# A fourth slot for the 0/1 adjacency, made in the round's second unit in place of its fifth

## The chip, the cores and the metric

The kernel runs on one core of one Trainium2 chip. Its metric is device time in microseconds (us). TensorE multiplies matrices (PE in the profile, its weight loads PEld), VectorE (DVE), ScalarE (ACT) and GpSimd (POOL) work element by element, and SyncE (SP) only issues transfers. Each engine runs its own list of instructions in order and waits on semaphores for the others.

## The reference

There are 16 graphs (batches) of 512 nodes with 128 features. A first stage mixes neighbours with the row-normalised adjacency, adds the input and normalises; five gated layers then pass messages over the 0/1 adjacency; a last residual and normalisation follow.

```python
adj_norm = adj / (jnp.sum(adj, axis=-1, keepdims=True) + EPS)
h = relu(concat([x, adj_norm @ x]) @ weight + bias)
x = layernorm(x + h)
A = (adj != 0).astype(x.dtype)
h = x
for l in range(5):
    m = h @ weight[l]
    agg = einsum('bij,bid->bjd', A, m)
    h = gru_cell(agg, h, w_ih, w_hh, b_ih, b_hh)   # gates r, z, n; h = (1 - z) * n + z * h
x = layernorm(x + h * mask)
```

## The kernel before

**Units and rounds.** One layer of one batch is a unit. A round (a `window` in the code) has five slots, and three batches are in flight: `UNITS = ((0, 0), (1, 2), (2, 4), (0, 1), (1, 3))` gives for each slot (rounds back, layer). So the first unit of a round is layer 0 of the youngest batch, the second layer 2 of the batch before, and so on. Beside its five units a round prepares the next batch (its first stage) and finishes an old one (its last normalisation, from round 3 on). Rounds -1, 0 and 1 are the ramp and have an order of their own; rounds 3 to 14 are one loop body, run twelve times; four rounds at the end are written out again. Every engine's list is written by hand inside `window`, slot by slot, and nothing else sets the order.

**A unit, by engine.** PE adds up the neighbours: four matmuls of `edges` with `tok_hi` (L1001) and four with `tok_lo` (L1006) into `ps_tok`. It then makes nine matmuls of the state with the recurrent weights into `ps_hn`, `ps_r`, `ps_z` (the helper at L893 to L895, called by `state_products`), turns the next unit's state into `ps_tok` (four transposes, L888) and makes nine matmuls of the aggregate with the input weights (L893 to L895 again). ACT takes `agg_hi` out of `ps_tok`, DVE makes `agg_lo` from it (L661), ACT makes `r_gate` (L635) and `z_gate` (L645), DVE `r_hn` (L874) and `n_pre` (L774), ACT `n_gate` (L573), POOL `z_h` (L495), DVE `zm_n` (L807) and the new `h` (L829). ACT rounds `h` to `h_hi`, POOL makes the rest `h_lo` (L485, for a new batch L490). DVE's tail of a unit (`n_pre`, `zm_n`, `h`) stands at the start of the next slot. Before the turn PE waits for `agg_lo`; before the aggregation it waits for `tok_lo`, and for a layer 0 also for the batch's `edges`, `x1_hi` and `x1_lo`.

**The 0/1 adjacency.** `edges_of` (L733) writes `edges` in four pieces of 128x512 from `adj_in` (`not_equal` 0) with DVE, into a ring of three slots, one for each batch in flight: slot `batch % RING`. In the rounds from 2 on it stands behind `h` in the fifth slot (slot 4), after the old batch's last aggregation has been waited for. In the ramp it stands in other places. PE takes the ring's slots of the batches in flight by three numbers (`ring`).

**Around the new place.** In slot 1 of a round DVE makes, behind `h`: the four pieces of `pre2` (L744), four `stats2` (L760), `row_eps` (128x4, L847), `mv2` (L753), `var2` (128x4, L755), then `tok_lo` of the unit in slot 2 (L661). ACT reads `adj_in` for the row sums in the same slot (L542). In slot 0 DVE also makes `xt_lo` (L661), and POOL `adjt_lo` (L438) behind `z_h`.

**Transfers.** SP loads, in this order in a round, the next inputs `xt_in` (after `xt_lo`) and `adjt_in` (after `adjt_lo`), stores the finished output, loads `x_in` (after `pre1`), and last `adj_in`, after the row sums and `edges`.

Of the kernel before, what the change touches and what calls it, by code (L numbers as in the profile page):

```python
# [22 lines left out]
LAST = UNITS.index((2, LAYERS - 1))  # L23
# [151 lines left out]
def program(nc, x, xt, adj, adjt, mask, w0, b0, wlt, wiht, whht, gru_b, out):  # L175
    B, N, D = x.shape
    C = N // P
# [3 lines left out]
    with ExitStack() as ctx:  # L181
        def sb(name, shape, dtype=F32):
            return ctx.enter_context(nc.sbuf_tensor(name, shape, dtype))
# [4 lines left out]
        def sem(name):  # L188
            return ctx.enter_context(nc.semaphore(name))
# [24 lines left out]
        adjt_in = sb("adjt_in", [P, C, N])  # L214
        xt_in = sb("xt_in", [P, N])
        x_in = sb("x_in", [P, C, D])
        RING, KEPT = 3, 4
        edges = sb("edges", [P, RING, C, N], F32R)
        x1_kept = sb("x1_kept", [P, KEPT, C, D])

# [56 lines left out]
        s_adj_in = sem("s_adj_in")  # L277
# [42 lines left out]
        s_agg = sem("s_agg")  # L320
# [337 lines left out]
        def _(dve):  # L658
# [9 lines left out]
            def weights():  # L668
                dve.wait_ge(s_small, 2 * 16)
                nc.vector.tensor_tensor(rz_bias[:], bih_cols[:, 0:2], bhh_cols[:, 0:2], ALU.add).then_inc(s_whh, 1)  # L670
                dve.wait_ge(s_weights, 3 * 16)
                nc.vector.tensor_copy(whh_hi[:], whh_t[:]).then_inc(s_whh, 1)
                dve.wait_ge(s_whh, 2)
                low_part(whh_lo[:], whh_t[:], whh_hi[:]).then_inc(s_whh, 1)
                for l in range(LAYERS):
                    dve.wait_ge(s_wc_hi, l + 1)
                    low_part(wc_lo[:, l, :], product_bank[l][:, 0:G * D], wc_hi[:, l, :]).then_inc(s_wc_lo, 1)

            def window(w):
# [15 lines left out]
                def mean_parts():  # L695

                    dve.wait_ge(s_nsum_tok, w.prepared(1, 1))
                    dve.wait_ge(s_rinv, w.prepared(2, 2))
                    for c in range(C):
                        last = nc.vector.scalar_tensor_tensor(  # L700
                            out=mixed[:, c, :], in0=ps_b[0][:, c * D:(c + 1) * D],
                            scalar=row_inv[:, c:c + 1], in1=own[:, c, :], op0=ALU.mult, op1=ALU.add)
                    last.then_inc(s_mixed, 1)
# [16 lines left out]
                def moments1():  # L720

                    for c in range(C):
                        nc.vector.bn_aggr(mv1[:, c, :], stats1[:, c, :]).then_inc(s_mv1, 1)
                    dve.wait_ge(s_mv1, w.prepared(C, C))
                    nc.vector.tensor_scalar(var1[:], mv1[:, :, 1], LN_EPS, None, ALU.add).then_inc(s_var1, 1)  # L725
# [5 lines left out]
                def edges_of(cs):  # L731
                    for c in cs:
                        nc.vector.tensor_scalar(edges[:, bass.ds(ring, 1), c, :].rearrange("p o m -> p (o m)"),  # L733
                                                adj_in[:, c, :], 0.0, None, ALU.not_equal).then_inc(s_edges, 1)
# [28 lines left out]
                if w.prepares():  # L763
                    ring = dve.snap(w.batch(-1) % RING)
# [3 lines left out]
                for slot in range(SLOTS):  # L768
# [57 lines left out]
                    if w.unit_before(slot):  # L826
                        dve.wait_ge(s_zh, w.units(slot))
                        dve.wait_ge(s_zm1n, w.units(slot))
                        nc.vector.tensor_tensor(h[made][:], z_h[:], zm1_n[:], ALU.subtract).then_inc(s_h, 1)  # L829
                    if w.first == -1 and slot == 1:  # L830
                        weights()
                    if w.prepares():
                        if slot == 2 and not w.leads():
                            mean_parts()
                        if slot == 3 and not w.ramps():
                            moments1()
                        if slot == 4 and not w.ramps():

                            dve.wait_ge(s_agg, w.units(LAST + 1))
                            edges_of(range(C))  # L840
                    if slot == 1 and w.finishes() and not w.idles():
                        pre2_of_batch()
                        if slot == w.end_slot():
# [34 lines left out]
                    if slot == 1 and w.ramps() and w.first != 0:  # L878

                        edges_of(range(2) if w.first == -1 else range(C))  # L880

            all_windows(window, dve)


        @block.tensor
        def _(pe):
# [21 lines left out]
            def window(w):  # L908
# [37 lines left out]
                    gs = slice(g * D, (g + 1) * D)  # L946
                    return split_product(dst[:], weights_hi[:, gs], weights_lo[:, gs], hi[:], lo[:], start, stop)

                ring = [pe.snap(w.batch(back) % RING) if w.first - back >= 0 else None for back in range(RING)]

                def edges_from(c, back):

# [31 lines left out]
                for slot in range(SLOTS):  # L984
# [72 lines left out]
                    if slot == 1 and w.leads():  # L1057
                        sums_by_tokens()
                        if w.first == -1:
# [4 lines left out]
                            own_products(1)  # L1064

            all_windows(window, pe)


# [34 lines left out]
```

## Time and profile before

| | us |
|---|---|
| median of 3 runs | 680.66 |
| lowest and highest | 679.27, 681.64 |
| profiled execution, span from first to last instruction | 678.2 |
| PE busy | 621.9 (92%) |
| DVE busy | 568.8 (84%) |
| ACT busy | 416.0 (61%) |
| POOL busy | 390.5 (58%) |
| one round in the loop (the same instruction of two rounds, 320.79 and 360.09) | 39.3 |

The profiled span is 2.5 us under the median of the runs; a sum made on the trace is carried over to the median by adding that. The granted TensorE clock of the span is 0.984 of full speed, and 1.00 in the rounds that are looked at below. In a timeline a duration includes the time that an issued instruction is held at an operand, so one form of instruction with two durations is a sign of being held.

### The profile page before, as it was taken

Reading aid. Unit: us, or ns where it says so; the run is one execution under the profiler, and the core shown is the slowest. Engines: PE = TensorE matmul, PEld = TensorE weight load, DVE = VectorE, ACT = ScalarE, POOL = GpSimd, SP = SyncE. Lnnn points to the kernel's source line nnn. Section 1 sums busy time; section 2 is a strip of 40 time slices with the busy share of each in tenths; the row PEclk is TensorE's granted clock in tenths of the full one; section 3 lists DMA queues with packets and bytes.
Section 4 is the critical chain, followed back from the end, with each engine's and each line's share of the span. In section 5 each row is a group of like instructions: output and inputs, shape, how many; then the busy total and the mean of one; then the engine's idle time right before and its main releaser. Section 6 shows DMA issues by size and latency. Waiting matters only on the chain.

```text
span 678.2 us, 10100 instructions
## 1 busy us (share of the span) xinstructions
PE 621.9 (92%) x2922; PEld 496.0 (73%) x2922; DVE 568.8 (84%) x1153; ACT 416.0 (61%) x775; POOL 390.5 (58%) x309
## 2 busy tenths in 40 slices
PE   4588899999999999999999999999999999999973
PEld 3467677787877778787777878777787878778852
DVE  1867877989899898989989898998989899886664
ACT  3557385766757576675757667575766667555431
POOL 3526373664757566475767657566765747546252
PEclk9799999999999999999999999999999999999987
DMA  7351302221212222221222221131222111000001
GB/s 226 132 163 40 116 17 78 79 78 51 104 31 84 86 77 77 69 86 31 96 75 77 77 84 71 31 113 57 77 77 92 62 31 62 15 0 16 1 16 31
DMA packets 37424, 47.28 MB, mean 70 GB/s; under 512 B 1409, under 2 KB 18945, under 8 KB 37409
## 3 DMA queue, kind: packets, MB, share of 16 engines
q1 hardware_dynamic: 36368, 46.27, 20.5%
q10 hardware_dynamic: 944, 0.72, 0.3%
q0 software_dynamic: 96, 0.10, 0.2%
q8 instruction: 7, 0.11, 0.1%
q14 instruction: 9, 0.07, 0.0%
HBM read 42.90 MB, written 4.19 MB: 69 GB/s over the span
## 4 chain that ended last, share of the span: by engine, by line
PE 57%; DVE 28%; issue 9%; ACT 4%; DMA 2%; DVEq 1%; POOLq 0%; SPq 0%; ACTq 0%
PE ps_tok L1001 8%; PE ps_tok L1006 7%; DVE edges L733 5%; PE ps_tok L888 4%; DVE r_hn L874 3%; PE ps_r L893 3%; PE ps_r L894 3%; PE ps_b L894 3%; PE ps_b L893 3%; PE ps_r L895 3%; PE ps_b L895 3%; PE ps_z L893 3%; PE ps_z L895 3%; PE ps_z L894 3%; DVE zm_n L807 3%
## 5 line engine op out<-in xcount | busy, mean ns | idle before, releaser
L485 POOL TENSOR_TENSOR h_lo<-h,h_hi 128x512 fp32r<-128x512 f32 x64 | 84.2, 1315 | 108.2 <-ACT h_hi L522 108.2
L495 POOL TENSOR_TENSOR z_h<-z_gate,h 128x512 f32<-128x512 f32 x80 | 104.8, 1310 | 47.2 <-ACT z_gate L645 47.2
L438 POOL TENSOR_TENSOR adjt_lo<-adjt_in,adjt_hi 128x512 fp32r<-128x512 f32 x64 | 95.1, 1508 | 31.3 <-ACT adjt_hi L522 31.3
L1001 PE MATMUL ps_tok<-edges,tok_hi 128*128 (+1 forms) x320 | 92.2, 411 | 17.7 <-DVE edges L733 15.3
L522 ACT ACTIVATE tok_hi<-ps_tok 128x512 fp32r<-128x512 f32 x64 | 38.3, 599 | 108.6 <-PE ps_tok L888 108.5
L573 ACT ACTIVATE n_gate<-n_pre,gru_bias 128x512 f32<-128x512 f32 x80 | 57.7, 722 | 63.4 <-DVE n_pre L774 63.4
L1006 PE MATMUL ps_tok<-edges,tok_lo 128*128 (+1 forms) x320 | 88.4, 399 | 0.0
L1001 PEld LDWEIGHTS ps_tok<-edges,tok_hi 128*128 128x128 f32 x320 | 59.0, 191 | 38.7 <-issue 22.9
L829 DVE TENSOR_TENSOR h<-z_h,zm_n 128x512 f32<-128x512 f32 x80 | 85.2, 1065 | 0.8
L807 DVE SCALAR_TENSOR_TENSOR zm_n<-z_gate,n_gate 128x512 f32<-128x512 f32 x80 | 66.2, 828 | 22.1 <-ACT n_gate L573 20.1
L874 DVE SCALAR_TENSOR_TENSOR r_hn<-ps_hn,gru_bias,r_gate 128x512 f32<-128x512 f32 x80 | 59.5, 744 | 27.2 <-ACT r_gate L635 27.0
L1006 PEld LDWEIGHTS ps_tok<-edges,tok_lo 128*128 128x128 f32 x320 | 60.8, 190 | 14.7
L522 ACT ACTIVATE h_hi<-h 128x512 fp32r<-128x512 f32 x80 | 50.2, 628 | 20.9 <-DVE h L829 20.7
L635 ACT ACTIVATE r_gate<-ps_r,rz_bias 128x512 f32<-128x512 f32 x80 | 54.9, 687 | 12.4 <-PE ps_r L895 9.7
L774 DVE TENSOR_TENSOR n_pre<-ps_in,r_hn 128x512 f32<-128x512 f32 x80 | 55.3, 692 | 8.1
L661 DVE TENSOR_TENSOR tok_lo<-ps_tok,tok_hi 128x512 fp32r<-128x512 f32 x64 | 44.1, 688 | 19.7 <-ACT tok_hi L522 19.4
L522 ACT ACTIVATE agg_hi<-ps_tok 128x512 fp32r<-128x512 f32 x80 | 48.0, 600 | 19.5 <-PE ps_tok L1006 18.5
L661 DVE TENSOR_TENSOR agg_lo<-ps_tok,agg_hi 128x512 fp32r<-128x512 f32 x80 | 54.5, 682 | 3.7 <-ACT agg_hi L522 3.4
L645 ACT ACTIVATE z_gate<-ps_z,rz_bias 128x512 f32<-128x512 f32 x80 | 55.1, 689 | 0.4
L444 POOL TENSOR_TENSOR rstd<-var,minus_half 128x4 f32<-128x4 f32 x16 | 16.2, 1011 | 55.8 <-DVE var L725 55.7
L888 PE MATMUL ps_tok<-ident,h 128*128 128x128 f32 x256 | 39.9, 278 | 9.0 <-DVE h L829 7.3
L888 PEld LDWEIGHTS ps_tok<-ident,h 128*128 128x128 f32 x256 | 29.4, 140 | 24.2 <-DVE agg_lo L661 9.5
(123 smaller groups left out, 1603.3 us busy)
## 6 DMA issues: line engine op xcount, KB each, us to landing
adjt_in<-in_adj_t_dram SPq DMA_DIRECT2D x16, 1024.0 KB, 5.2
adj_in<-in_adj_dram SPq DMA_DIRECT2D x16, 1024.0 KB, 5.2
xt_in<-in_x_t_dram SPq DMA_DIRECT2D x16, 256.0 KB, 2.8
x_in<-in_x_dram SPq DMA_DIRECT2D x16, 256.0 KB, 2.7
out_dram<-y_out SPq DMA_DIRECT2D x16, 256.0 KB, 2.3
wl_t<-in_wl_t_dram ACTq DMA_DIRECT2D x1, 320.0 KB, 5.4
wih_t<-in_w_ih_t_dram ACTq DMA_DIRECT2D x1, 192.0 KB, 3.0
whh_t<-in_w_hh_t_dram ACTq DMA_DIRECT2D x1, 192.0 KB, 9.3
```

What stands on the lines that cost most here:

```text
L438: nc.gpsimd.tensor_tensor(adjt_lo[:, j, :], adjt_in[:, j, :], raw(adjt_hi[:, j, :]), ALU.subtract).then_inc(s_adjt_lo, 1)
L485: nc.gpsimd.tensor_tensor(h_lo[made][:], h[made][:], raw(h_hi[made][:]), ALU.subtract).then_inc(s_h_lo, 1)
L495: nc.gpsimd.tensor_tensor(z_h[:], z_gate[:], h[layer][:], ALU.mult).then_inc(s_zh, 1)
L522: return nc.scalar.activation(dst, src, ACT.Copy)
L661: return nc.vector.tensor_tensor(dst, src, raw(hi), ALU.subtract)
L807: nc.vector.scalar_tensor_tensor(out=zm1_n[:], in0=z_gate[:], scalar=1.0, in1=n_gate[:], op0=ALU.subtract, op1=ALU.mult).then_inc(s_zm1n, 1)
L829: nc.vector.tensor_tensor(h[made][:], z_h[:], zm1_n[:], ALU.subtract).then_inc(s_h, 1)
L874: nc.vector.scalar_tensor_tensor(out=r_hn[:], in0=ps_hn[:], scalar=bhh_cols[:, 2:3], in1=r_gate[:], op0=ALU.add, op1=ALU.mult).then_inc(s_ ...
L888: return nc.tensor.transpose(dst, src, ident[:])
L893: nc.tensor.matmul(dst, lhs_hi, rhs_hi, start=start, stop=False)
L1001: nc.tensor.matmul(ps_tok[:], tok_hi[:, c * P:(c + 1) * P], edges_from(c, unit[0]), start=c == 0, stop=False)
L1006: last = nc.tensor.matmul(ps_tok[:], tok_lo[:, c * P:(c + 1) * P], edges_from(c, unit[0]), start=False, stop=c == C - 1)
```

## The change

The ring `edges` gets four slots. In the rounds from 2 on, DVE writes the next batch's `edges` in slot 1, behind `h` and ahead of `pre2`, where it stood in slot 4 behind `h`. What it waits for changes with it: for the load of `adj_in` by name, and for the last aggregation of the batch that had the ring's slot before, which was in the round before. PE still takes three numbers of the ring, now modulo 4. SP's order of transfers is not touched.

```diff
-        RING, KEPT = 3, 4
+        RING, KEPT = 4, 4
...
+                    if w.prepares() and slot == 1 and not w.ramps():
+
+                        dve.wait_ge(s_adj_in, w.prepared(16, 16))
+                        if w.first >= 3:
+                            dve.wait_ge(s_agg, w.last_layers())
+                        edges_of(range(C))
...
-                        if slot == 4 and not w.ramps():
-
-                            dve.wait_ge(s_agg, w.units(LAST + 1))
-                            edges_of(range(C))
...
-                ring = [pe.snap(w.batch(back) % RING) if w.first - back >= 0 else None for back in range(RING)]
+                ring = [pe.snap(w.batch(back) % RING) if w.first - back >= 0 else None for back in range(3)]
```

DVE's list in the loop, slot 1, before:

```order
L829 TENSOR_TENSOR h<-z_h,zm_n 128x512 [waits s_zm1n,s_zh]
L738 REGISTER_ALU
L744 ISA [waits s_cent2,s_x1_kept,s_last]
L744 SCALAR_TENSOR_TENSOR pre<-ps_b,mask_cols,x_kept 128x128
```

and now:

```order
L829 TENSOR_TENSOR h<-z_h,zm_n 128x512 [waits s_zm1n,s_zh]
L832 ISA
L834 REGISTER_ALU [waits s_adj_in]
L733 ISA [waits s_agg]
L733 TENSOR_SCALAR edges<-adj_in 128x512
L733 ISA
L733 TENSOR_SCALAR edges<-adj_in 128x512
L733 ISA
L733 TENSOR_SCALAR edges<-adj_in 128x512
L733 ISA
L733 TENSOR_SCALAR edges<-adj_in 128x512
L738 REGISTER_ALU
```

The four pieces of `edges` now stand between `h` and `pre2`, and so ahead of `row_eps`, `var2` and the `tok_lo` of slot 2. DVE's list at the end of the loop body, slot 4, before:

```order
L829 TENSOR_TENSOR h<-z_h,zm_n 128x512 [waits s_zm1n,s_zh]
L733 ISA [waits s_agg]
L733 TENSOR_SCALAR edges<-adj_in 128x512
L733 ISA
L733 TENSOR_SCALAR edges<-adj_in 128x512
L733 ISA
L733 TENSOR_SCALAR edges<-adj_in 128x512
L733 ISA
L733 TENSOR_SCALAR edges<-adj_in 128x512
L874 SCALAR_TENSOR_TENSOR r_hn<-ps_hn,gru_bias,r_gate 128x512 [waits s_r]
```

and now:

```order
L661 TENSOR_TENSOR agg_lo<-ps_tok,agg_hi 128x512 [waits s_agg_hi]
L829 TENSOR_TENSOR h<-z_h,zm_n 128x512 [waits s_zm1n,s_zh]
L876 SCALAR_TENSOR_TENSOR r_hn<-ps_hn,gru_bias,r_gate 128x512 [waits s_r]
```

There `r_hn` follows `h` directly. The lists of PE, ACT, POOL and SP keep their order.

## Rows read from the trace of the kernel before

**Rows 1.** The page's first part: busy time, share of the span, instructions.

```profile
PE 621.9 (92%) x2922; PEld 496.0 (73%) x2922; DVE 568.8 (84%) x1153; ACT 416.0 (61%) x775; POOL 390.5 (58%) x309
```

**Rows 2.** Waits of the whole span: who waited for whom, us, times, longest.

```profile
PEld ps_tok L1001 <- issue: 22.9, 24, 1.7
...
PE ps_tok L1001 <- DVE edges L733: 15.3, 13, 1.2
```

**Rows 3.** Timeline of PE, round's end and next slot 0: start, us, instruction.

```profile
348.34 1.09 PE L1001 MATMUL ps_tok<-edges,tok_hi 128*128 x4
...
350.20 0.39 PE L893 MATMUL ps_hn<-h_hi,whh_hi 128*128 128x512 f32 x1
...
361.31 0.39 PE L895 MATMUL ps_in<-agg_hi,wc_lo 128*128 128x512 f32 x1
362.89 1.19 PE L1001 MATMUL ps_tok<-edges,tok_hi 128*128 x4 [1.19 <-DVE edges L733]
...
364.85 0.39 PE L893 MATMUL ps_hn<-h_hi,whh_hi 128*128 128x512 f32 x1
...
366.92 0.65 PE L888 MATMUL ps_tok<-ident,h 128*128 128x128 f32 x4
```

**Rows 4.** Timeline of DVE over the same slot 0.

```profile
358.64 1.53 DVE L829 TENSOR_TENSOR h<-z_h,zm_n 128x512 f32<-128x512 f32 x1
360.09 2.50 DVE L733 TENSOR_SCALAR edges<-adj_in 128x512 f32 x4
362.52 0.74 DVE L874 SCALAR_TENSOR_TENSOR r_hn<-ps_hn,gru_bias,r_gate 128x512 f32<-128x512 f32 x1
...
363.97 1.62 DVE L661 TENSOR_TENSOR xt_lo<-xt_in,xt_hi 128x512 fp32r<-128x512 f32 x1
365.51 0.68 DVE L807 SCALAR_TENSOR_TENSOR zm_n<-z_gate,n_gate 128x512 f32<-128x512 f32 x1
366.12 0.68 DVE L661 TENSOR_TENSOR agg_lo<-ps_tok,agg_hi 128x512 fp32r<-128x512 f32 x1
```

**Rows 5.** Timeline of ACT over the same slot 0.

```profile
361.22 0.68 ACT L635 ACTIVATE r_gate<-ps_r,rz_bias 128x512 f32<-128x512 f32 x1
...
362.88 0.63 ACT L522 ACTIVATE xt_hi<-xt_in 128x512 fp32r<-128x512 f32 x1
364.09 0.72 ACT L573 ACTIVATE n_gate<-n_pre,gru_bias 128x512 f32<-128x512 f32 x1 [0.57 <-DVE n_pre L774]
```

**Rows 6.** Timeline of POOL over the same slot 0.

```profile
360.91 1.40 POOL L485 TENSOR_TENSOR h_lo<-h,h_hi 128x512 fp32r<-128x512 f32 x1 [1.29 <-ACT h_hi L522]
362.50 1.29 POOL L490 TENSOR_TENSOR h_lo<-h,h_hi 128x512 fp32r<-128x512 f32 x1 [0.18 <-ACT h_hi L522]
363.74 1.31 POOL L495 TENSOR_TENSOR z_h<-z_gate,h 128x512 f32<-128x512 f32 x1
```

**Rows 7.** The lines of `edges` at 360 and `adjt_lo` at 333: min/median/max ns.

```profile
L733 DVE TENSOR_SCALAR edges<-adj_in x4: 411/412/1493, 360.1 to 361.1; 128x512 f32 x4
...
L438 POOL TENSOR_TENSOR adjt_lo<-adjt_in,adjt_hi x2: 1283/1511/1739, 333.2 to 334.4; 128x512 fp32r<-128x512 f32 x2
```

**Rows 8.** Timeline of all engines, slot 1 and the start of slot 2.

```profile
333.51 1.51 DVE L807 SCALAR_TENSOR_TENSOR zm_n<-z_gate,n_gate 128x512 f32<-128x512 f32 x1
...
336.64 1.11 DVE L744 SCALAR_TENSOR_TENSOR pre<-ps_b,mask_cols,x_kept 128x128 f32<-128x128 f32 x4
...
338.79 0.17 DVE L847 TENSOR_SCALAR row_eps<-row_sum 128x4 f32<-128x4 f32 x1
...
339.24 1.29 POOL L485 TENSOR_TENSOR h_lo<-h,h_hi 128x512 fp32r<-128x512 f32 x1 [3.07 <-ACT h_hi L522]
339.27 1.28 DVE L755 TENSOR_SCALAR var<-mv 128x4 f32<-128x4 f32 x1
...
340.47 0.68 DVE L661 TENSOR_TENSOR tok_lo<-ps_tok,tok_hi 128x512 fp32r<-128x512 f32 x1
```

**Rows 9.** Timeline of PE and of its weight loads there.

```profile
341.10 0.39 PE L895 MATMUL ps_in<-agg_hi,wc_lo 128*128 128x512 f32 x1
341.34 1.19 PE L1001 MATMUL ps_tok<-edges,tok_hi 128*128 x4
...
341.33 0.53 PEld L1001 LDWEIGHTS ps_tok<-edges,tok_hi 128*128 128x128 f32 x3 [0.28 <-issue]
```

## The prediction

> **What bounds the kernel now.** I read the page's busy times first: PE is busy for 621.9 of 678.2 us [rows 1], so the end can only come earlier by way of PE's gaps. The waits come second. In the middle of the run one gap has the change's name on it: PE waits for `edges` 13 times, 15.3 us in all, once for each `edges` that is made in a slot 4 [rows 2]. The timelines of one round come third. PE issues the last matmul of slot 4 at 361.31; the next one would follow 0.24 later, at 361.55, as matmuls of this form do in a row (341.10 to 341.34 in [rows 9]). It begins at 362.89 [rows 3], so the gap costs 1.34 us a round, and 13 of them 17.4 us. That is the most that this edit can give back at this place.
>
> **Part 1: the gap in slot 0.** With `edges` gone from DVE's list, PE begins the aggregation at 361.55. Its eight matmuls take 1.86 us (348.34 to 350.20 [rows 3]), so it is at the state products at 363.41. There it needs the new batch's `h_lo` from POOL, which ends at 362.50 + 1.29 = 363.79 [rows 6]. That `h_lo` follows ACT's chain behind DVE's `h`, which ended ahead of `edges`, so it comes no earlier. PE begins the state products at about 363.87, against 364.85, and has them done 2.07 later (364.85 to 366.92 [rows 3]), at 365.94. The turn that follows waits for `agg_lo`, and here the gain is lost. Line by line:
> - `r_hn` waits for `r_gate`, which ends at 361.22 + 0.68 = 361.90 [rows 5]; it starts at 361.96 in place of 362.52 [rows 4]. Only 0.56 us of the 2.50 us of `edges` comes back, since ACT was not ready.
> - `xt_lo` comes 1.45 behind `r_hn` (362.52 to 363.97), so at 363.41, but `xt_hi` ends at 363.51 [rows 5]: 363.55.
> - Now DVE and POOL meet. In [rows 8] `zm_n` takes 1.51 us where it takes 0.68 in [rows 4], under POOL's first `adjt_lo`, and POOL's second one takes 1.739 us where the first took 1.283 [rows 7]. So DVE's instruction was held until the first ended, went next, and held the second for 0.46. They take turns. By this `xt_lo`, queued at 363.55, goes when `h_lo` ends at 363.79, and is done at 364.33 (in the trace it ended 0.54 after the end of `z_h`: 363.97 + 1.62 against 363.74 + 1.31). `z_h` is held for 0.46 and ends at 365.51 instead of 365.05.
> - `n_gate` takes 0.72 [rows 5] and is ready at 364.27; `zm_n` comes when `z_h` is already next in turn, so it is held until 365.51 and ends some 0.56 later, 366.07, against 366.19 before. `agg_lo` follows 0.61 behind: 366.68 against 366.80 [rows 4].
> So PE turns at 366.80 instead of 366.92: **0.12 us a round**. If `z_h` goes ahead of `xt_lo`, both are as before and the gain is 0. Were DVE never held behind `z_h`, `agg_lo` would be done before 365.94 and the gain 366.92 - 365.94 = 0.98. I take 0.12, the value that the turns in [rows 7, 8] give, and keep 0 and 0.98. For 13 rounds: -1.6 us (0 to -12.7).
>
> The Trainium skill ("SBUF — State Buffer", section "Who interferes with whom") says that VectorE and GpSimd share one pair of ports by an exclusive lock for an instruction with two SBUF inputs or in a two-port mode, and that the one that issues first keeps it to its end. The held `zm_n` agrees with that. By that rule `zm_n` can't pass `z_h`, and the gain of this part is the 0.12 or 0.
>
> **Part 2: `edges` in slot 1.** It stands behind `h`, so from 336.64, where `pre2` starts now [rows 8]. Of the four pieces in [rows 7] three take 0.41 us; the fourth, 1.49 us, is held by POOL's `h_lo` at 360.91. The pieces start 0.34 apart (360.1 to 361.1 for four), so four that are not held push back what follows by 1.36 us. POOL is idle here until its `h_lo` at 339.24 (3.07 us idle before it [rows 8]), so they are not held, and cost 1.36 instead of 2.50. The two waits in front of them are for things long done: the load of `adj_in`, which ACT reads earlier in the same slot, and an aggregation of the round before. Behind them in DVE's list stand `pre2`, `stats2`, `row_eps`, `mv2`, `var2` and `tok_lo`.
> - `row_eps` moves from 338.79 to 340.15. POOL's `h_lo` runs from 339.24 to 340.53. `var2`, the same operation and size, took 1.28 us under it where `row_eps`, ahead of it, took 0.17 [rows 8]; now `row_eps` is the one that is held, until 340.53, and ends at about 340.65, 1.69 later than now (338.96).
> - `mv2` follows, and `var2` comes when POOL is idle and takes 0.17 instead of 1.28. Now `tok_lo` ends at 340.47 + 0.68 = 341.15. From `row_eps` to `var2` it is 0.48 (338.79 to 339.27); counted from 340.57, where the held one would have started unheld, `var2` is at about 341.0, `tok_lo` starts 0.1 behind it and ends at 341.75. So 1.1 of the 1.69 us disappears in the wait of `var2`, which was there anyway, and **0.60 us** is left.
> - PE waits for this `tok_lo`. Its weight load for slot 2 starts at 341.33, after a gap of 0.28, and 0.18 behind `tok_lo`; the matmul before was issued at 341.10 and the next is due at 341.34 [rows 9]. There is no slack. The 24 gaps in the row of [rows 2] that says "issue" are two for each of 12 rounds, 1.91 a round: one in slot 0 and this one. So a later `tok_lo` delays PE one for one.
> Only rounds with `pre2` in slot 1, 3 to 14, have this queue: 12 x 0.60 = +7.2 us. The bounds are 0.27 if the small `row_eps` is not held after all (`var2` then starts at 340.63 and `tok_lo` ends at 341.42) and 0.9 if `cent2` and `y_out` of POOL in slot 2 also come to lie before DVE's `zm_n` and `h` and delay the next `tok_lo`: 12 x 0.27 = +3.2, 12 x 0.9 = +10.8. I take 0.60, by the row of the held `var2`.
>
> What of it comes back later in the round? PE has no other gap in slots 2 to 4 that is larger than some 0.2 us, and DVE's later chain hangs on PE's turn in slot 2 by way of `tok_hi` and `r_gate`, so both are late by the same amount when slot 0 comes. Nothing is given back.
>
> **Part 3: what costs nothing.** The ring of four needs memory, not time; PE's list keeps its order and its three register numbers. The `adj_in` load can leave right behind the `x_in` load in slot 3 instead of in the next slot 0. Nobody waits for it in either place: its next reader is a slot 1. It would lie beside other work, and I count 0. The Trainium skill (same page, section "SBUF: two separate sides") says that a transfer can't be slowed by a compute operation nor the other way round. The same 0 would result; no row here isolates it.
>
> **The sum.** -1.6 + 7.2 = +5.6 us on the profiled 678.2: 683.8. The median of the runs lies 2.5 above that span, so 686.3 us, which is 0.8% more. The measurement tells about 0.3%, or 2 us, from no change.
>
> **Rivals.**
> 1. *The gap really closes (faster).* If DVE's `zm_n` gets in ahead of `z_h`, slot 0 gives 0.98 a round, 12.7 in all, and even with the cost of part 2 it is 680.66 - 12.7 + 7.2 = 675.2. For it speaks that `n_gate` is ready at 364.27, just when `xt_lo` ends; against it that `z_h` is by then queued for half a microsecond, and the held and holding pairs of [rows 7, 8]. From a gain of 0.72 a round on (12 x 0.60 + 2.0 over 13) the kernel is faster.
> 2. *The cost in slot 1 is mostly hidden (no change).* If a 128x4 `row_eps` slips through under `h_lo`, the cost is 3.2 and the sum +1.6: 682.3. Against it stands `var2` at 1.28 us, for it that this one starts in the middle of POOL's instruction and not 0.03 behind its start.
> 3. *More than one `tok_lo` is late (slower still).* DVE's `zm_n` in slot 2 slides behind POOL's `cent2` and its `h` behind `y_out`; then `tok_lo` of slot 3 is late too. At 0.9 a round and no gain in slot 0 it is +10.8: 691.5.
> 4. *The edit doesn't do what it says.* PE would go on waiting for `edges` 13 times. The order of DVE's list excludes it: the pieces are 20 us ahead of their reader. I give it none.
>
> **Chances.** Forecast 0.60, rival 1 0.16, rival 2 0.14, rival 3 0.10. The forecast's own range, with 0 to 0.12 in slot 0 and 0.5 to 0.7 in slot 1, is 685 to 689. The range for 8 in 10 reaches down to rival 1 and up to near rival 3: 675 to 690. Slower by over 0.3%: forecast, rival 3 and no more, less a little for a forecast that falls short: 0.67. Within: 0.17. Faster: 0.16.
>
> **What would show it.** In the profile after, PE's wait for `edges` is gone; in its place PE waits in slot 0 for POOL's `h_lo` (0.4 to 0.5 us) and before the turn for `agg_lo` (about 0.9 us), and `z_h` of slot 0 takes 1.7 to 1.8 us instead of 1.31. In slot 1 four `edges` take about 0.41 us each, `row_eps` about 0.5 us or is seen as held, `var2` 0.17, and PE's gap ahead of slot 2 grows from 0.28 to 0.8 or 0.9. The round is 39.8 us long instead of 39.3. I am wrong if `zm_n` in slot 0 ends less than 1.6 us after PE's state products began (2.2 by the forecast, 1.0 by rival 1), or if the gap ahead of slot 2 does not grow.

## The result and the profile after

The changed kernel takes 685.26 us in the median (684.75 to 686.6, four runs), the kernel before 681.07 in the same runs; the ratio is 1.0079 with a 95% interval of 1.0057 to 1.0101. It is slower by 4.2 us in the medians; the interval allows 3.9 to 6.9 us. The profiled execution spans 683.7 us against 678.2.

First the busy times and PE's waits over the whole span (us, times, longest).

```profile
PE 628.1 (92%) x2922; PEld 497.3 (73%) x2922; DVE 556.0 (81%) x1153; ACT 414.2 (61%) x775; POOL 397.2 (58%) x309
```

```profile
PE ps_tok L890 <- DVE agg_lo L661: 6.8, 13, 0.6
PE ps_tok L1003 <- DVE tok_lo L661: 6.3, 14, 1.4
PE ps_hn L895 <- POOL h_lo L490: 4.6, 13, 0.4
```

The 13 waits for `edges` of [rows 2] are gone, with 15.3 us. In their place stand two waits in slot 0, for `h_lo` and for `agg_lo`, and one in slot 2, for `tok_lo`. DVE is busy for 12.8 us less than in the kernel before, mainly since four `edges` take 1.42 us where they took 2.50, and the kernel is slower all the same. (The new code is two lines longer, so L888, L893, L1001 and L874 of before are L890, L895, L1003 and L876 here.)

Slot 0, on PE, then DVE, then POOL, to be laid beside [rows 3, 4, 6]:

```profile
365.17 1.10 PE L1003 MATMUL ps_tok<-edges,tok_hi 128*128 x4
...
367.56 0.49 PE L895 MATMUL ps_hn<-h_hi,whh_hi 128*128 128x512 f32 x1 [0.36 <-POOL h_lo L490]
...
370.41 0.65 PE L890 MATMUL ps_tok<-ident,h 128*128 128x128 f32 x4 [0.51 <-DVE agg_lo L661]
```

```profile
365.57 0.75 DVE L876 SCALAR_TENSOR_TENSOR r_hn<-ps_hn,gru_bias,r_gate 128x512 f32<-128x512 f32 x1 [1.76 <-ACT r_gate L635]
...
367.18 0.79 DVE L661 TENSOR_TENSOR xt_lo<-xt_in,xt_hi 128x512 fp32r<-128x512 f32 x1
...
367.90 1.78 DVE L807 SCALAR_TENSOR_TENSOR zm_n<-z_gate,n_gate 128x512 f32<-128x512 f32 x1
```

```profile
366.13 1.29 POOL L490 TENSOR_TENSOR h_lo<-h,h_hi 128x512 fp32r<-128x512 f32 x1 [0.29 <-ACT h_hi L522]
...
367.39 1.74 POOL L495 TENSOR_TENSOR z_h<-z_gate,h 128x512 f32<-128x512 f32 x1
```

PE begins the aggregation on time (365.17), and turns 5.24 us later. Before, the matmul was due at 361.55 and the turn began at 366.92, 5.37 us later [rows 3]. So 0.13 us is gained where 1.34 us of gap was taken away. DVE now idles 1.76 us ahead of `r_hn`; `xt_lo` is queued under POOL's `h_lo` and goes ahead of `z_h`; `z_h` takes 1.74 us, and `zm_n`, held behind it, takes 1.78 where it takes 0.68 when nothing holds it.

Slot 1 and the start of slot 2, all engines but PE, then PE's weight loads one round later, beside [rows 8, 9]:

```profile
339.75 1.42 DVE L733 TENSOR_SCALAR edges<-adj_in 128x512 f32 x4
341.09 1.11 DVE L744 SCALAR_TENSOR_TENSOR pre<-ps_b,mask_cols,x_kept 128x128 f32<-128x128 f32 x4
...
342.36 1.29 POOL L485 TENSOR_TENSOR h_lo<-h,h_hi 128x512 fp32r<-128x512 f32 x1 [3.07 <-ACT h_hi L522]
...
343.24 0.43 DVE L849 TENSOR_SCALAR row_eps<-row_sum 128x4 f32<-128x4 f32 x1
...
343.99 0.17 DVE L755 TENSOR_SCALAR var<-mv 128x4 f32<-128x4 f32 x1
344.08 0.69 DVE L661 TENSOR_TENSOR tok_lo<-ps_tok,tok_hi 128x512 fp32r<-128x512 f32 x1
```

```profile
384.64 0.76 PEld L1003 LDWEIGHTS ps_tok<-edges,tok_hi 128*128 128x128 f32 x4 [0.79 <-issue]
```

`edges` pushes back `pre2` by 1.34 us. `row_eps` is the one that is held now (0.43 us), `var2` is free (0.17 in place of 1.28), and PE's gap ahead of the aggregation of slot 2 is 0.79 us instead of 0.28: 0.51 us more.

-0.13 + 0.51 = +0.38 us a round. The round can be measured by itself at ACT's copy `x_kept`, which runs once in each. Of the kernel after it is, from first to last of eleven:

```profile
L522 ACT ACTIVATE x_kept<-x x11: 622/624/625, 163.2 to 560.3; 128x512 f32 x11
```

That is 397.1 us for ten rounds, 39.71 each. Before, the same view has

```profile
L522 ACT ACTIVATE x_kept<-x x12: 622/623/625, 161.5 to 594.3; 128x512 f32 x12
```

432.8 us for eleven rounds, 39.35 each. Unrounded the difference is 0.364 us. The twelve rounds of the loop take 12 x 0.364 = 4.4 us longer, and the medians differ by 4.2. The profiled spans differ by 5.5; the rest lies in the ramp, which the change does not touch. The first two copies are 18.9 us apart in the trace of before (29.6 to 48.5), 20.6 after, and 21.0 in the first experiment, which has the ramp of before. The control below, which has the change, has 18.9 too. The granted TensorE clock from 30 to 50 us is 0.95 and 0.94 of full speed in the two traces with 18.9, and 0.84 in that of after and of the first experiment. So this piece is the scatter of the start, and the trace of before had a short one.

### The profile page after: what moved, and what is told of

Same layout as the page of the kernel before. It is cut to its first block, busy times and chain, and to the rows that moved or that the text cites. A ratio compares the mean times of both kernels' runs of the same rounds, so it can differ in the third digit from the quotient of the medians.

```text
span 683.7 us, 10112 instructions
## 1 busy us (share of the span) xinstructions
PE 628.1 (92%) x2922; PEld 497.3 (73%) x2922; DVE 556.0 (81%) x1153; ACT 414.2 (61%) x775; POOL 397.2 (58%) x309
## 4 chain that ended last, share of the span: by engine, by line
DVE 37%; PE 31%; issue 17%; ACT 12%; DVEq 2%; DMA 1%; ACTq 0%; POOLq 0%; SPq 0%
DVE h L829 5%; PE ps_tok L1003 4%; PE ps_tok L1008 4%; DVE r_hn L876 3%; DVE zm_n L807 3%; PE ps_tok L890 3%; DVE tok_lo L661 3%; ACT z_gate L645 3%; DVE edges L733 3%; DVE x L709 3%; DVE pre L716 2%; DVE pre L744 2%; ACT adjt_hi L522 2%; DVE agg_lo L661 2%; DVE n_pre L774 2%
## 5 line engine op out<-in xcount | busy, mean ns | idle before, releaser
L495 POOL TENSOR_TENSOR z_h<-z_gate,h 128x512 f32<-128x512 f32 x80 | 110.1, 1377 | 49.8 <-ACT z_gate L645 49.8
L438 POOL TENSOR_TENSOR adjt_lo<-adjt_in,adjt_hi 128x512 fp32r<-128x512 f32 x64 | 100.6, 1594 | 16.2 <-ACT adjt_hi L522 16.2
L807 DVE SCALAR_TENSOR_TENSOR zm_n<-z_gate,n_gate 128x512 f32<-128x512 f32 x80 | 89.2, 1116 | 22.2 <-ACT n_gate L573 20.3
L876 DVE SCALAR_TENSOR_TENSOR r_hn<-ps_hn,gru_bias,r_gate 128x512 f32<-128x512 f32 x80 | 59.6, 746 | 47.6 <-ACT r_gate L635 47.4
L1003 PE MATMUL ps_tok<-edges,tok_hi 128*128 (+1 forms) x320 | 91.5, 409 | 6.4 <-DVE tok_lo L661 6.3
L1008 PE MATMUL ps_tok<-edges,tok_lo 128*128 (+1 forms) x320 | 89.9, 404 | 0.0
L829 DVE TENSOR_TENSOR h<-z_h,zm_n 128x512 f32<-128x512 f32 x80 | 83.6, 1045 | 0.8
L1003 PEld LDWEIGHTS ps_tok<-edges,tok_hi 128*128 128x128 f32 x320 | 59.9, 191 | 25.6 <-issue 9.8
L890 PE MATMUL ps_tok<-ident,h 128*128 128x128 f32 x256 | 40.1, 279 | 15.3 <-DVE h L829 7.4
L890 PEld LDWEIGHTS ps_tok<-ident,h 128*128 128x128 f32 x256 | 29.4, 141 | 32.5 <-issue 14.1
```

What stands on the lines that cost most here:

```text
L438: nc.gpsimd.tensor_tensor(adjt_lo[:, j, :], adjt_in[:, j, :], raw(adjt_hi[:, j, :]), ALU.subtract).then_inc(s_adjt_lo, 1)
L495: nc.gpsimd.tensor_tensor(z_h[:], z_gate[:], h[layer][:], ALU.mult).then_inc(s_zh, 1)
L807: nc.vector.scalar_tensor_tensor(out=zm1_n[:], in0=z_gate[:], scalar=1.0, in1=n_gate[:], op0=ALU.subtract, op1=ALU.mult).then_inc(s_zm1n, 1)
L876: nc.vector.scalar_tensor_tensor(out=r_hn[:], in0=ps_hn[:], scalar=bhh_cols[:, 2:3], in1=r_gate[:], op0=ALU.add, op1=ALU.mult).then_inc(s_ ...
L890: return nc.tensor.transpose(dst, src, ident[:])
L1003: nc.tensor.matmul(ps_tok[:], tok_hi[:, c * P:(c + 1) * P], edges_from(c, unit[0]), start=c == 0, stop=False)
```

## The experiments

My theory: the gap in slot 0 was only the uppermost of several things that end at the same moment (DVE and POOL take turns there), and the whole loss is that `edges` stands ahead of the `tok_lo` for which PE waits. The rivals: the ring or an earlier transfer costs something by itself; the bound of slot 0 is another one (ACT's chain, `h_lo`); the two places share one bound. All ratios are to the kernel before, in the same runs, where its median was 680.4 to 681.1 us; a difference of two medians out of different rows carries that scatter, and the round's length does not.

| kernel | median us | ratio (95% interval) | one round, us |
|---|---|---|---|
| before | 681.07 | | 39.35 |
| changed | 685.26 | 1.0079 (1.0057 to 1.0101) | 39.71 |
| ring of four alone | 681.07 | 1.0001 (0.9987 to 1.0015) | 39.35 |
| changed, `row_eps` ahead | 681.39 | 1.0004 (0.9987 to 1.0022) | 39.45 |
| changed, moments behind | 677.47 | 0.9941 (0.9923 to 0.9959) | 39.08 |
| changed, `xt_lo` behind | 688.76 | 1.0109 (1.0079 to 1.0140) | 39.88 |
| changed, `xt` early | 679.59 | 0.9976 (0.9962 to 0.9990) | 39.23 |
| changed, both mends | 671.66 | 0.9869 (0.9846 to 0.9891) | 38.62 |
| changed, loop shorter by a round | 684.19 | 1.0054 (1.0033 to 1.0076) | 39.69 |
| before, moments behind | 680.0 | 0.9981 (0.9969 to 0.9994) | 39.23 |
| both mends, `edges` in slot 4 | 693.0 | 1.0167 (1.0134 to 1.0199) | 40.29 |

**The ring alone.** `RING` is 4 and `ring` has three numbers; nothing else.

```diff
-        RING, KEPT = 3, 4
+        RING, KEPT = 4, 4
```

> The kernel before with the ring of four slots alone; `edges` stays in slot 4. My theory (the whole loss is `edges` standing ahead of `tok_lo` in slot 1): no change, within 0.3% of before, PE still waits for `edges` 13 times for 15.3 us, round 39.3 us. The rival (the ring, its memory or its register arithmetic costs something by itself): part of the 4 to 5 us is seen here, 2 us or more.

681.07 us, ratio 1.0001. PE's waits read as before:

```profile
PE ps_tok L1001 <- DVE edges L733: 15.3, 13, 1.2
```

The ring costs nothing. What is left is the move, with the earlier load of `adj_in` that it allows.

**`row_eps` ahead of `pre2`.** Behind `edges`, before POOL's `h_lo` begins; `row_inv` takes its old place.

```diff
+                    ahead = slot == 1 and w.prepares() and w.finishes()
+                    if ahead:
+                        dve.wait_ge(s_row_sum, w.prepared(C, C))
+                        nc.vector.tensor_scalar(row_eps[:], row_sum[:], ROW_EPS, None, ALU.add).then_inc(s_rinv, 1)
                     if slot == 1 and w.finishes() and not w.idles():
                         pre2_of_batch()
```

> The changed kernel, but in the rounds with `pre2` in slot 1 `row_eps` stands behind `edges` and ahead of `pre2`, before POOL's `h_lo` starts, and `row_inv` where `row_eps` stood. My theory: `row_eps` is no longer held (0.17 us in place of 0.43), `tok_lo` of slot 2 ends 0.2 to 0.37 us earlier, 12 rounds, 2.4 to 4.4 us less than the changed kernel: 681 to 683 us. The rival (the cost of slot 1 is the 1.36 us of `edges` as such, not what POOL holds): no difference from the changed kernel, 685 us.

681.39 us, 3.9 us under the changed kernel. The timeline of slot 1:

```profile
340.51 0.16 DVE L846 TENSOR_SCALAR row_eps<-row_sum 128x4 f32<-128x4 f32 x1
...
341.76 1.29 POOL L485 TENSOR_TENSOR h_lo<-h,h_hi 128x512 fp32r<-128x512 f32 x1 [3.07 <-ACT h_hi L522]
...
342.63 0.18 DVE L853 RECIPROCAL row_inv<-row_eps 128x4 f32<-128x4 f32 x1
...
344.09 0.76 PEld L1010 LDWEIGHTS ps_tok<-edges,tok_hi 128*128 128x128 f32 x4 [0.51 <-issue]
```

One instruction on four columns is not held any more, and PE's gap shrinks from 0.79 to 0.51, the round by 0.26 us (12 x 0.26 = 3.1 us, of the 3.9 in the medians). `row_inv`, of the same size, now stands in the old place of `row_eps`, in the middle of `h_lo`, and is not held: 0.18 us, in all 11 rounds that were looked at. So it is not the place alone: what stands in it has to be an instruction that `h_lo` holds. The work of `edges` is the same. So of the 0.36 us that a round lost, 0.26 hang on what POOL's `h_lo` holds, and the place of one small instruction decides it.

**Moments behind `tok_lo`.** `row_eps`, `mv2` and `var2` stand behind it in rounds 3 to 14.

```diff
-                    if w.prepares() and slot == 1:
+                    behind = slot == 1 and w.prepares() and w.finishes()
+                    if w.prepares() and slot == 1 and not behind:
...
-                        moments2()
+                        if not behind:
+                            moments2()
...
+                    if behind:
+                        dve.wait_ge(s_row_sum, w.prepared(C, C))
+                        nc.vector.tensor_scalar(row_eps[:], row_sum[:], ROW_EPS, None, ALU.add).then_inc(s_rinv, 1)
+                        moments2()
```

> The changed kernel, but `row_eps`, `mv2` and `var2` stand behind `tok_lo` of slot 2 instead of ahead of it (rounds 3 to 14). My theory: `tok_lo` ends about 0.9 us earlier, PE's wait for it in slot 2 (0.52 us a round) is gone, 12 x 0.52 = 6.2 us less than the changed kernel: about 679 us, 2 us under before, round 39.1 to 39.2. The rival (the lost time sits in slot 0 or in a transfer that leaves earlier): the round stays at 39.7 us.

677.47 us, 0.6% under before and 7.8 under the changed kernel; somewhat more than expected. The timelines of DVE and of PE:

```profile
339.68 0.69 DVE L661 TENSOR_TENSOR tok_lo<-ps_tok,tok_hi 128x512 fp32r<-128x512 f32 x1
340.28 0.16 DVE L870 TENSOR_SCALAR row_eps<-row_sum 128x4 f32<-128x4 f32 x1
```

```profile
340.63 0.39 PE L903 MATMUL ps_in<-agg_hi,wc_lo 128*128 128x512 f32 x1
340.86 1.10 PE L1009 MATMUL ps_tok<-edges,tok_hi 128*128 x4
```

`tok_lo` ends at 340.37 and PE goes on 0.23 us behind its last matmul: no gap at all. The four matmuls take 1.10 instead of the 1.19 of [rows 9], so the kernel before also lost about 0.1 us a round at this place. That was the part that I had not counted.

**`xt_lo` behind `agg_lo`.** It takes DVE's `xt_lo` out of the queue between POOL's `h_lo` and `z_h`, and nothing else.

```diff
-                        if slot == 0 and w.makes_parts():
+                        if slot == 0 and w.makes_parts() and w.first < 2:
                             xt_lo_of_batch()
...
                         low_part(agg_lo[:], ps_tok[:], agg_hi[:]).then_inc(s_agg_lo, 1)
+                    if slot == 0 and w.makes_parts() and w.first >= 2:
+                        xt_lo_of_batch()
```

> The changed kernel, but DVE makes `xt_lo` of slot 0 behind `agg_lo` instead of ahead of `zm_n`. My theory (in slot 0 `xt_lo` goes between POOL's `h_lo` and `z_h`, which holds `z_h` and so `zm_n` and `agg_lo`): `z_h` takes 1.30 in place of 1.74 us, `zm_n` and `agg_lo` end 0.45 us earlier and PE turns 0.4 to 0.5 us earlier; part or all of it is lost again, since PE's next products wait for the later `xt_lo`. Total between 679 and 688 us; the decisive number is the time from PE's last matmul of slot 4 to its turn in slot 0, 5.24 us in the changed kernel, 4.8 by my theory. The rival (ACT's chain and POOL's `h_lo` alone set the turn): 5.24 stays.

688.76 us, just above the expected 679 to 688. The timelines of POOL, DVE and PE in slot 0:

```profile
329.41 1.30 POOL L495 TENSOR_TENSOR z_h<-z_gate,h 128x512 f32<-128x512 f32 x1
```

```profile
329.94 1.32 DVE L807 SCALAR_TENSOR_TENSOR zm_n<-z_gate,n_gate 128x512 f32<-128x512 f32 x1 [0.79 <-ACT n_gate L573]
...
331.78 1.17 DVE L661 TENSOR_TENSOR xt_lo<-xt_in,xt_hi 128x512 fp32r<-128x512 f32 x1
```

```profile
327.20 1.10 PE L1005 MATMUL ps_tok<-edges,tok_hi 128*128 x4
...
331.99 0.65 PE L892 MATMUL ps_tok<-ident,h 128*128 128x128 f32 x4
...
333.00 0.39 PE L897 MATMUL ps_b<-w_hi,xt_hi 128*128 128x256 f32 x1 [0.36 <-DVE xt_lo L661]
```

`z_h` is back at 1.30 us and PE turns at 4.79 us where the changed kernel needs 5.24. ACT and `h_lo` were the same, so they were not the bound. The time is lost again at once: the products that need `xt_lo` begin 1.01 us behind the turn and wait for it, where they follow directly in the changed kernel (0.41, 370.41 to 370.82). In total it is slower, 0.17 us a round, which is some 2 us of the 3.5 between the medians. The mechanism of slot 0 is shown.

**`xt` early.** ACT's `xt_hi` for the next round goes into slot 3, DVE's `xt_lo` behind `h` in slot 4, into the idle time that the moved `edges` left.

```diff
+                    if slot == 3 and w.leads_on():
+                        xt_hi_of_batch(w.after())
...
+                    if slot == 4 and w.leads_on():
+                        xt_lo_of_batch(w.after())
```

`leads_on` is true for rounds 2 to 13, and `after` is the next round.

> The changed kernel, but ACT makes `xt_hi` for the next round in slot 3, where it idles 2.19 us, and DVE `xt_lo` behind `h` in slot 4, where `edges` used to stand and DVE now idles 1.76 us (rounds 2 to 13, for rounds 3 to 14; for that the loop runs one round less and round 14 is written out). My theory: nothing of DVE goes between POOL's `h_lo` and `z_h` in slot 0, `z_h` takes 1.30 us, `agg_lo` and PE's turn come 0.45 us earlier, and nobody waits for `xt_lo`: 12 x 0.45 = 5.4 us less than the changed kernel, 680 us, round 39.25. The rival (ACT's chain and `h_lo` set slot 0): PE's turn stays at 5.24 us behind the last matmul of slot 4 and the time at 685.

679.59 us, 5.7 under the changed kernel and 4.6 under the control that follows. POOL's and DVE's timelines:

```profile
363.30 1.28 POOL L503 TENSOR_TENSOR z_h<-z_gate,h 128x512 f32<-128x512 f32 x1
```

```profile
359.64 0.68 DVE L671 TENSOR_TENSOR xt_lo<-xt_in,xt_hi 128x512 fp32r<-128x512 f32 x1
361.48 0.75 DVE L888 SCALAR_TENSOR_TENSOR r_hn<-ps_hn,gru_bias,r_gate 128x512 f32<-128x512 f32 x1 [1.16 <-ACT r_gate L645]
```

`xt_lo` takes 0.68 us, nothing holds it, and 1.16 us of idle time is left. The round is 0.48 us shorter, as `z_h` is (0.46).

**The control.** The loop one round shorter and round 14 written out, which the last run and the next need.

```diff
-            with eng.Fori(0, B - 4) as trip:
+            with eng.Fori(0, B - 5) as trip:
```

> The changed kernel with the loop one round shorter and round 14 written out, nothing else: the control for the two runs above. All theories: no difference from the changed kernel, 685 us. If it is off, what it is off by has to be taken from those two.

684.19 us, and a round of 39.69 against 39.71. The median is 1.1 us below the changed kernel's, and the two intervals overlap; the round says that the shorter loop gives nothing.

**Both mends.**

> Both mends at once: `row_eps`, `mv2`, `var2` behind `tok_lo` in slot 1, `xt_hi` in slot 3 and `xt_lo` in slot 4. If the two terms are independent, as my theory has them, the gains add: 677.5 - 5.4 = 672 us, 1.3% under before, round 38.6. If they share one bound (DVE's chain as a whole), less than half of the second is seen: 675 us or more.

671.66 us, 1.3% under the kernel before; the best kernel of this study. From the changed kernel it is 13.6 us, and the two single gains are 7.8 and 5.7. Measured from the control, as both kernels with `xt` early have its loop, it is 12.5 against 7.8 + 4.6. They add either way, so the two places do not share a bound. PE and DVE in slot 0:

```profile
319.45 1.10 PE L1021 MATMUL ps_tok<-edges,tok_hi 128*128 x4
...
321.84 0.50 PE L913 MATMUL ps_hn<-h_hi,whh_hi 128*128 128x512 f32 x1 [0.36 <-POOL h_lo L498]
...
324.23 0.65 PE L908 MATMUL ps_tok<-ident,h 128*128 128x128 f32 x4
```

The turn is at 4.78 us. The wait for `h_lo`, 0.36 us as in the changed kernel, is now the larger gap of slot 0.

**The kernel before with the moments behind.** The same edit as above, on the ring of three with `edges` in slot 4.

> The kernel before (ring of three, `edges` in slot 4) with `row_eps`, `mv2` and `var2` behind `tok_lo` of slot 2. My theory: `tok_lo` there was late by 0.09 us a round only (aggregation of 1.95 in place of 1.86 us), so 1.1 us less than before, 679.8 us; then of the 3.4 us that the changed kernel with this order has under before, 2 to 2.5 us come from the gap in slot 0 (0.12 to 0.2 a round). The rival (the order alone gives the gain, and moving `edges` gives none): the same 677.5 us.

680.0 us, 1.1 under before, as expected to 0.2. The order by itself is worth 1.1 us, the order with the move 3.4 (intervals of the ratios 0.9969 to 0.9994 and 0.9923 to 0.9959). So the move of `edges` brings some 2.5 us when it doesn't stand in the way of `tok_lo`; a round is 39.08 against 39.23. In this kernel `row_eps` takes 1.14 us, held by `h_lo`, and it costs nothing that can be seen, since the `tok_lo` for which PE waits is already made.

**Both mends without the move.** `edges` in slot 4, `xt_lo` behind it, a ring of three.

> Both mends, but with `edges` left in slot 4 and a ring of three; `xt_lo` stands behind `edges`. It asks whether the move of `edges` is worth something once what came in its way is gone. My theory (`edges` and `xt_lo` need the same 1.76 us in which DVE waits for `r_gate`, and only one fits): `xt_lo` is queued at 2.5 us behind `h`, under POOL's second `h_lo`, and pushes `r_hn`, `zm_n` and `agg_lo` back, PE turns 0.5 to 1.0 us later than before, 686 to 692 us against 671.7 with the move. The rival (the two mends carry the gain, and the place of `edges` is indifferent): 672 to 676 us.

693.0 us, a little above the expected 686 to 692. DVE and PE:

```profile
367.75 2.51 DVE L743 TENSOR_SCALAR edges<-adj_in 128x512 f32 x4
370.18 1.80 DVE L671 TENSOR_TENSOR xt_lo<-xt_in,xt_hi 128x512 fp32r<-128x512 f32 x1
371.90 0.74 DVE L892 SCALAR_TENSOR_TENSOR r_hn<-ps_hn,gru_bias,r_gate 128x512 f32<-128x512 f32 x1
```

```profile
370.55 1.20 PE L1019 MATMUL ps_tok<-edges,tok_hi 128*128 x4 [1.19 <-DVE edges L743]
...
375.65 0.55 PE L906 MATMUL ps_tok<-ident,h 128*128 128x128 f32 x3 [0.62 <-DVE agg_lo L671]
```

`xt_lo` is held for over a microsecond by POOL's second `h_lo`, everything behind it is late, and PE waits twice. With the move the two mends bring 13.6 us against the changed kernel, and without it they cost 12.6 us against the kernel before in the same runs. The moments alone bring 1.1 us there, so it is `xt_lo` that costs. The room in slot 4 is the larger yield of the change, beside the 2.5 us that it brings by itself; the change puts nothing there. That `xt_lo` needs this room is not shown: DVE of the kernel before also idles 0.79 us ahead of `zm_n` in slot 2, and no kernel with `edges` in slot 4 had `xt_lo` there.

## Why the prediction was right

The forecast was 686.3 us, the measured median is 685.26. On the trace's own time it was 683.8 against 683.7, but that close a meeting is partly luck: 1.1 us of it is the scatter of the ramp, and the mechanism is worth +4.2 to +4.4 us where the sum had +5.6. The 2.5 us between span and median were partly scatter as well: the profiled execution of the kernel after has 683.7 us of span and 685.5 of time, 1.8 apart, and the rest of the 2.5 came from a profiled execution of before that was 0.7 us under the median.

- **The gap in slot 0 (part 1).** 0.12 us a round was forecast, 0.13 measured. Every step is in the trace: PE's wait for `h_lo` (0.36, forecast 0.4 to 0.5), `xt_lo` ahead of `z_h`, `z_h` at 1.74 us, `zm_n` behind it. Counted from the start of the aggregation `agg_lo` ends at 5.11 us, by the forecast at 5.13. Only PE's wait for it is shorter than the 0.9 us that was forecast, 0.51: the state products began 0.07 us later than forecast and took 2.18 us in place of 2.07. That cost nothing, as `agg_lo` sets the turn. The turn-taking of DVE and POOL was read from `adjt_lo` at 1283 and 1739 ns [rows 7], and taking `xt_lo` out of it moved the turn by 0.45 us, as it should.
- **The cost in slot 1 (part 2).** 0.60 us a round was forecast, 0.51 measured. The mechanism holds: `edges` pushes by 1.34 (forecast 1.36), `row_eps` is held instead of `var2`, PE has no slack. Two small sizes in the term were off. From the start of `row_eps` to that of `tok_lo` it is 0.84 us, not 0.92: the held `row_eps` took 0.43 us. So 12 x 0.51 = 6.1 us and not 7.2.
- **What costs nothing (part 3).** The ring alone changes nothing (1.0001). That the earlier `adj_in` load is free was not isolated. It is issued at 354.93, right behind that of `x_in` (354.39), takes 5.5 us to land in the median where it took 5.2, and its first reader comes some 22 us after the issue; the kernel with both mends has the same early load and is the fastest.
- **The sum.** -0.13 x 13 + 0.51 x 12 = +4.4 us, which is what the twelve rounds show.
- **Rival 1 (the gap closes)** (whose border with no change is a gain of 0.71 a round, not 0.72) is excluded: `zm_n` ended 2.1 us behind the start of the state products (367.90 + 1.78 against 367.56), not 1.0. **Rival 2 (`row_eps` slips through)** as well: it was held. The experiment that puts it out of the way shows that the rival's price was about right: PE's gap is then 0.51 against 0.28, a cost of 0.23 us where the rival had 0.27. **Rival 3 (the next `tok_lo` too)** did not come about: `zm_n` in slot 2 did slide behind `cent2` (1.45 us), but the 14 waits for `tok_lo` are one for each of the 12 rounds and two at the ends that every kernel here has (2.0 to 2.4 us together), so none is left for slot 3. **Rival 4** is excluded by the waits.

The Trainium skill's exclusive lock ("SBUF — State Buffer", section "Who interferes with whom") agrees with these held instructions, down to one on 4 columns that is held for a quarter of a microsecond (0.43 against 0.16 to 0.17 us). One pair of rows of the kernel before does not fit it; there the measurement decides:

```profile
342.84 1.01 POOL L451 TENSOR_TENSOR rstd<-var,minus_half 128x4 f32<-128x4 f32 x1
```

```profile
343.45 0.69 DVE L807 SCALAR_TENSOR_TENSOR zm_n<-z_gate,n_gate 128x512 f32<-128x512 f32 x1 [0.79 <-ACT n_gate L573]
```

`zm_n` starts in the middle of POOL's instruction and is not held. Why is open; POOL's spans are rough.

## What to carry to other kernels

A gap with one name on it is an upper bound: before removing its cause, follow the other inputs of the next two waits and see when each of them would have been there. Here 1.34 us of gap held 0.13 us of gain. Work that is moved to an idle engine still stands ahead of something; look for the next result in that engine's list for which the bounding engine waits with no slack, and put the filler behind that. A change that loses can still have made room: count what the vacated place can take before dropping it.

## What the runs showed of the hardware

DVE and POOL take turns instruction by instruction when both are queued: DVE's instruction goes when POOL's current one ends, and POOL's next one takes 0.44 to 0.46 us longer (1283 to 1739 ns for `adjt_lo`, 1.30 to 1.74 us for `z_h`), which is less than the 0.68 us that DVE's instruction takes by itself. So an instruction of DVE can delay a later one of its own by way of POOL. What holds is not a matter of size: under POOL's `h_lo` the 128x4 `TENSOR_SCALAR` instructions `var2` (kernel before) and `row_eps` (changed kernel) took 1.28 and 0.43 us in place of 0.17. Under it too, the 128x4 reciprocal `row_inv` took 0.18 us with `row_eps` ahead, and `tok_lo` of 128x512, which reads one of its inputs from `ps_tok`, its usual 0.69 with the moments behind (339.68, `h_lo` from 338.78 to 340.07). I had not expected how much hangs on four columns: moving `row_eps` (0.17 us of work) ahead of the eight instructions of `pre2` and `stats2` was worth 3.9 us of the whole kernel in the medians, 3.1 by the rounds.
